# Attention on one Trainium2 core: scores ahead of the V products in each slot of TensorE's order

## The reference

```python
q = _rope((xn @ q_w + q_b)...)          # (b, heads, 1024, 64)
k = _rope((xn @ k_w + k_b)...)
v = (xn @ v_w + v_b)...
scores = einsum('bhqd,bhkd->bhqk', q, k) * scale
scores = where(causal, scores, -inf)
attn = softmax(scores, axis=-1)
ctx = einsum('bhqk,bhkd->bhqd', attn, v)
attn_out = ctx @ o_w + o_b + xn
```

## Time and profile before

| | us |
|---|---|
| median of 3 runs | 2389.39 |
| lowest, highest | 2388.45, 2394.24 |
| profiled execution | 2398.74 |
| its span, first to last instruction | 2396.8 |

### The profile page before, as it was taken

One profiled execution on the slowest core, in us unless ns is written; L12 is line 12 of the kernel. 1 busy time (PEld: TensorE's weight loads), 2 busy tenths in 40 slices (PEclk: granted clock), 3 DMA queues, 4 the chain that ended last, 5 costly groups with the idle time before them and its releaser, 6 DMA issues.

```text
span 2396.8 us, 42183 instructions
## 1 busy us (share of the span) xinstructions
PE 1980.7 (83%) x9942; PEld 1306.6 (55%) x9942; DVE 1684.5 (70%) x3031; ACT 1446.2 (60%) x2909; POOL 889.7 (37%) x907
## 2 busy tenths in 40 slices
PE   3759999879785999978967699996996669998798
PEld 1236666557324666655732566664672256665566
DVE  4867677569496676757948767674894877677488
ACT  2537777647453777755744477773674357776476
POOL 1554434133165343403316634431332554342222
PEclk8889999979797999998979899998897989999899
DMA  2011101011001011101100111100110011010011
GB/s 75 0 31 31 39 21 37 1 30 41 24 1 40 24 37 27 30 5 32 35 24 1 40 34 27 39 18 10 33 29 24 0 40 41 24 35 18 18 32 31
DMA packets 65411, 64.49 MB, mean 27 GB/s; under 512 B 12184, under 2 KB 48384, under 8 KB 65280
## 3 DMA queue, kind: packets, MB, share of 16 engines
q1 hardware_dynamic: 65280, 63.01, 10.0%
HBM read 27.31 MB, written 2.10 MB: 12 GB/s over the span
## 4 chain that ended last, share of the span: by engine, by line
PE 56%; DVE 21%; issue 12%; ACT 5%; POOL 2%; DVEq 1%; DMA 1%; ACTq 1%; SPq 0%; POOLq 0%
PE ps L1397 10%; PE ps L1236 6%; PE ps L1237 6%; PE ps L1238 6%; DVE state L966 5%; PE ps L1386 5%; PE ps L1376 5%; PE ps L1377 4%; PE ps L1412 3%; PE ps L1505 2%; PE ps L1264 2%; ACT ps L706 2%; DVE ps L1057 1%; DVE ctxT L1069 1%; DVE bx L959 1%
## 5 line engine op out<-in xcount | busy, mean ns | idle before, releaser
L741 ACT ACTIVATE probsT<-ps 128x512 f32<-128x512 f32 (+3 forms) x768 | 347.8, 490 | 262.6 <-PE ps L1386 262.6
L729 ACT ACTIVATE probs<-ps,least 128x640 f32<-128x640 f32 (+7 forms) x512 | 379.5, 741 | 67.4 <-DVE least L1052 58.0
L1376 PE MATMUL ps<-k_high,q_split 128*128 128x512 f32 (+3 forms) x768 | 312.2, 406 | 60.1 <-DVE q_split L1042 32.9
L1386 PE MATMUL ps<-ident,probs 128*128 128x128 f32 x2304 | 343.8, 277 | 12.9 <-ACT probsT L741 10.1
L1397 PE MATMUL ps<-probsT,vals 128*64 128x512 f32 (+3 forms) x1536 | 292.2, 504 | 9.3 <-ACT probsT L741 9.3
L1386 PEld LDWEIGHTS ps<-ident,probs 128*128 128x128 f32 x2304 | 272.3, 142 | 49.4 <-ACT probsT L741 24.9
L1059 DVE TENSOR_REDUCE least<-ps 128x1 f32<-128x640 f32 (+3 forms) x256 | 262.3, 1024 | 8.8
L1377 PE MATMUL ps<-k_low,q_split 128*128 128x512 f32 (+3 forms) x768 | 260.7, 352 | 0.0
L1376 PEld LDWEIGHTS ps<-k_high,q_split 128*128 128x128 f32 x768 | 148.0, 193 | 184.1 <-issue 100.0
L1052 DVE CUSTOM_DVE_ANT_0 ps<-ps,row_masks 128x128 f32<-128x128 f32 (+3 forms) x256 | 127.3, 498 | 166.4 <-PE ps L1377 163.3
L791 ACT ACTIVATE hid<-ps,cols 128x512 f32<-128x512 f32 x256 | 176.3, 689 | 104.1 <-PE ps L1238 75.9
(11 more groups left out here) (210 smaller groups left out, 4049.5 us busy)
## 6 DMA issues: line engine op xcount, KB each, us to landing
roped<-turned SPq DMA_DIRECT2D x512, 64.0 KB, 2.0
w<-in_w SPq DMA_DIRECT2D x128, 128.0 KB, 2.0
w_pair<-in_w_pairs SPq DMA_DIRECT2D x36, 128.0 KB, 2.6
xin<-in_x SPq DMA_DIRECT2D x5, 512.0 KB, 3.9
out<-acc SPq DMA_DIRECT2D x4, 512.0 KB, 4.1
pos<-in_c_pos SPq DMA_DIRECT2D x1, 512.0 KB, 4.9
v_w<-in_v_w SPq DMA_DIRECT2D x1, 512.0 KB
o_w<-in_o_w SPq DMA_DIRECT2D x1, 512.0 KB
```

The source lines that it names most:

```text
L729: act.activation(probs[:, t % 2, 0:width(t)], banks(2 * (t % 2))[:, 0:width(t)], ACT.Exp, bias=least[:, t:t + 1], scale=-1.0, accum_out=ro ...
L741: act.activation(dst, ps[:, T_BANK + g % 2, 0:k1 - k0], ACT.Copy).then_inc(t_taken, 1)
L1376: pe.matmul(o, q, k_high[par][h][:, k0:k1], start=True, stop=False)
L1386: made = pe.transpose(ps[:, T_BANK + g % 2, at - k0:at - k0 + P], probs[:, t % 2, at:at + P], ident[:, :])
```

## The change

In the slot loop of TensorE the two blocks that issue the V products move behind the block that issues the scores. In a slot with V products the order is now: side work, transposes of unit t - 1, scores of unit t + 2, V products. In slot 3 of the last pair `global_sums` also comes ahead of them. Slots without V products are as they were, and so is everything outside the loop.

```diff
@@ -1445,16 +1445,16 @@
                             turn_probs(n, t - 1)
                         elif not first:
                             turn_probs(n - 1, UNITS_A - 1)
-                        if t in PV_OLD_AT and not first:
-                            weigh_values(n - 1, 1 - par, 1, parts(TILES, PV_OLD_AT, t))
-                        if t in PV_NEW_AT:
-                            weigh_values(n, par, 0, parts(TPH, PV_NEW_AT, t))
                         if last and t == SUM_SLOT:
                             global_sums(b + 1, 1)
                         if t + 2 < UNITS_A:
                             scores(n, par, t + 2)
                         elif not last:
                             scores(n + 1, 1 - par, t + 2 - UNITS_A)
+                        if t in PV_OLD_AT and not first:
+                            weigh_values(n - 1, 1 - par, 1, parts(TILES, PV_OLD_AT, t))
+                        if t in PV_NEW_AT:
+                            weigh_values(n, par, 0, parts(TPH, PV_NEW_AT, t))
```

## The result

| | median, us | lowest, highest | runs |
|---|---|---|---|
| before | 2389.57 | 2388.45, 2394.24 | 4 |
| after | 2439.14 | 2435.03, 2440.68 | 4 |

The ratio is 1.02, with a 95% interval from 1.0183 to 1.0216: 44 to 52 us slower. It is not the quotient of the medians, which lie 49.6 us apart. One of the 17 later executions of the kernel before, with which experiments 5 to 8 are compared, took 2901.27 us at a mean granted clock of 0.64, and their ratios leave it out. The profiled execution of after took 2435.03 us, that of before 2398.74.

A forecast was written before the change was run, and what follows sets the result against it. TensorE was taken to bound a middle pair. Middle pairs +38.4, first pairs -2 and last pairs +7.6 gave +44 us on a median of 2389.39: 2433 us, with 8 in 10 between 2408 and 2450.

The forecast's parts named there:

- The slots: Middle pair, slots 1, 3, 5 and 7: scores moved ahead wait for the exponential, and the lateness accumulates to +2.82 us.
- the recursion: Middle pair: each slot's shift feeds the next exponential's end, giving +0.44, +0.93, +1.92 and +2.82 us at slots 1, 3, 5, 7.
- Give-backs: Middle pair: shrinking waits leave about +2.1 us after slot 10; slot 12's earlier scores return 0.8 us by slot 14.
- The drain: TensorE, between scores and V products: 0.17 us idle from the tiling mode change, as now seen behind the transposes.
- The rival without any drain: No drain between scores and V products: +22 us in all, 2412 us; chance 20%.
- The sum: Whole kernel: middle pairs 38.4, first pairs -2, last pairs +7.6, together +44 us.
- The prediction's own formula: Slot shift: end of exponential plus its own shift plus 0.05 plus 0.17, minus start of V products before.
- The last pair: V products no longer fill slot 3's wait for partial, 1.9 us; slots 5 and 7 add 0.5, slot 14 returns 0.5.
- Faster: Early scores win about 0.8 us a pair if the exponential of slot 3 ends before 324.65: 2375 us; chance 4%.
- Nothing changes: Scores of the same bank stay two slots apart, so waits might stay as they were: 2389 us; chance 3%.
- Give-backs fail: Lateness also reaches swaps, GpSimd's splits and the next pair's queries: up to +82, middle +65 us, 2454 us; chance 13%.

The follow-up runs named there:

- Experiment 5: Changed kernel, plus a third probs buffer and ScalarE's exponentials of units 3, 5 and 7 one slot earlier, ahead of a copy: 2405.71 us, ratio 1.0064.
- 6: Kernel before, plus a third probs buffer and ScalarE's exponentials of units 3, 5 and 7 one slot earlier: 2396.67 us, ratio 1.0031.
- experiment 7: Kernel before, with V products behind global_sums and the scores only in slot 3 of each sample's last pair: 2399.43 us, ratio 1.0043.
- 8: Kernel before, with slot 12's V products behind the scores, a third probs buffer and exponentials of units 3, 5 and 7 one slot earlier: 2373.12 us, ratio 0.9934.
- experiment 3: Kernel before, with V products moved behind the scores in slot 12 alone: 2368.64 us, ratio 0.9903.
- 2: Kernel before, with V products moved behind the scores only in slots 1, 3, 5 and 7: 2446.22 us, ratio 1.0227.
- 1: Kernel before, with V products moved behind the scores only in slots 11 and 12: 2383.32 us, ratio 0.996.
- experiment 4: Changed kernel, but the last pair of each sample keeps the old order in slots 1, 3, 5 and 7: 2418.68 us, ratio 1.0112.

## Why the prediction was right, step by step

- *The slots.* The pair of the earlier trace rows lengthens from one projection's start to the next by 0.36 (slots 0 and 1), 0.54 (2 and 3), 1.02 (4 and 5) and 0.93 (6 and 7), 2.85 us in all; the recursion gave +2.82 at the end of slot 7. It held because each exponential did move with the transposes of the slot before. Experiment 5 shows that step for slots 3, 5 and 7: with the exponential untied, slots 2 and 3 take 3.79 us and slots 4 and 5 take 4.03 us in the mean over the middle pairs, as before the change.
- *Give-backs.* Slots 8 to 10 returned 0.82 us (0.7 forecast). Slot 11 cost 0.23 (0.28). The wait for ctxT went, and slot 13 got 0.74 us shorter, but the scores in slot 14 then wait a little for the exponential of unit 14; slots 12 to 15 together gave back 0.68 us, as in experiment 3, where 0.8 was forecast. A middle pair, by the mean over all: +1.56 us against +1.6.
- *The drain.* The 0.17 us was right as a sum and wrong in its parts. The scores of slot 3 take 0.46 us (326.69 to 327.15 in the earlier trace rows); from 327.01 that ends at 327.47, and the V products start at 327.56, 0.09 later. Another 0.10 comes behind the V products: the first matmul of the projection there lasts 0.34 us to the next one (325.10 to 325.44), where it was 0.24 behind scores. (A first matmul behind a wait lasts as long, 0.34 us in slot 5 from 332.15, so this part is not peculiar to the V products.) The rival without any drain is out; the Trainium skill's rule (TensorEngine Tiling, Key Properties) that a change of tiling mode drains the engine agrees with the 0.09 us, and the trace gives no more than that for the step from scores to V products.
- *The sum.* In the two profiled executions, the first pairs (from their first scores to their spread in slot 12) grew from 111.6 to 114.0 us, the middle stretches from 913.8 to 951.2, and the last ones (from the spread of pair 6 to the last one) from 230.1 to 234.5: +44.3 us. Cut at the same places, the forecast's 44 is +1.1 (slot 11 alone, 4 x 0.28), +38.4 and +4.4 (4 x 1.9, less 4 x 0.8 for slots 12 to 15 of pair 6). Outside attention the profiled execution of before was 8 us longer than that of after, and it lay 9 us above its own median; nothing was changed there. That the traces give 44 to the microsecond is partly luck: the first stretch came out 1.4 us over its forecast and the middle one 1.0 us under it.
- *What was mis-sized.* The medians moved by 49.6 us, 5.6 more than forecast, and the interval of the ratio begins at 44. One term is shown to have been too small: slot 11 of the first pairs. The prediction takes its +0.28 from the rows of a middle pair, where the exponential of unit 11 ends 0.06 us behind the start of the V products. In the first pair of before it ends at 192.94 + 0.19 = 193.13, 0.95 us behind their start:

```profile
192.18 1.72 PE L1397 MATMUL ps<-probsT,vals 128*64 128x512 f32 x8
```

```profile
192.94 0.19 ACT L729 ACTIVATION_READ_ACCUMULATOR probs<-ps,least 128x1 f32 x1
```

The prediction's own formula gives 193.13 + 0.22 - 192.18 = +1.17 there. After the change the scores wait for it:

```profile
189.63 0.50 PE L1376 MATMUL ps<-k_high,q_split 128*128 128x512 f32 x1 [0.93 <-ACT probs L729]
```

From the V projection of slot 10 to the spread of slot 12, the first pairs take 5.7 us in every sample of before and of experiments 2, 3, 6, 7 and 8, and 6.8 us in every sample of after and of 1, 4 and 5, where slot 11 has the new order. That is +1.1 us a sample, 4.4 us in place of 1.1, so 3.3 us were missing there. (The summed first pairs of the two traces show only +2.5, because two samples of before had a longer stretch of low clock at their start, and sample 0 of after had no wait for the V sums in slot 10.)

- *The last pair.* The prediction has +2.4 us a sample for slots 1 to 7. From `global_sums` to the next spread, TensorE took 9.3 to 10.1 us in the trace of before and 12.2 to 12.5 after, +2.6 in the mean. The comparison with experiment 4 gives 3.8, of which some 1.3 is the clock. So no run shows that this term was too small. With the 3.3 us of the first pairs, and the middle pairs 1.0 us under their forecast, some 3 of the 5.6 us stay open; they are within the interval.
- *Faster* failed at the point named for it: the exponential of unit 3 did end behind the new place of the scores. But a part of that rival was true, and experiment 3 is that part alone.
- *Nothing changes* failed with the growth of the waits for the exponential, 3.7 to 15.4 us. *Give-backs fail* failed with +1.56 a pair.

## What to carry to other kernels

Before work is moved from ahead of a wait to behind it, read when the awaited event ends in the trace and what that event itself waits for: if it is tied to the engine that is being reordered, asking sooner does not make it come sooner, and each bare wait adds to the next. The same swap pays in a slot where the event is long over and something downstream is waiting, so it is worth testing slot by slot, not for a whole table. A term read in one place of the program holds for that place: the same slot cost 0.23 us in a middle pair and 1.1 us in a first pair. Work that stands in the cover of a long wait is free. Behind the wait it costs its time again: 1.9 us of V products cost 1.6 us a sample in the traces of experiment 7 and 2 to 2.5 by its runs, although the products themselves took 3.0 to 3.7 us at the low clock.

## What the runs showed of the hardware

- The change between matmuls of 128 and of 64 columns costs on both sides: 0.09 us from scores to V products, 0.10 us from V products to the next 128-column matmul (a first matmul behind a wait lasts as long), and 0.17 us from transposes to V products.
- The 1.2 GHz stretch behind the same wait of 4.4 us is not always equally long. The clock was back 4.7 to 6.6 us behind the wait in the four samples of before and 3.4 to 3.7 us behind it in experiment 4, with the same order of work there. Eight V product records at the same place of the program took 2.43 to 3.25 us in the one and 1.75 to 1.99 us in the other.
